# Four gather buffers instead of five, and a look-ahead of three units instead of four

## The reference

```python
x = x + _L0_conv_ref(_gn(x), ...)   # convs, scans over 1024, 256 and 64 positions, norms, gate
x = x + _L1_conv_ref(_gn(x), ...)   # 8 heads, softmax over 1024 positions
x = x + _L2_conv_ref(_gn(x), ...)   # deformable sampling, below
x = x + _L3_conv_ref(_gn(x))        # T = |u_i - u_j| * D, p <- T p twenty times, x * p
```

```python
samp = (v00 * (1 - wx) + v01 * wx) * (1 - wy) + (v10 * (1 - wx) + v11 * wx) * wy
return jnp.einsum('hwpc,hwp->hwc', samp, m)
```

## Time and profile before

| | us |
|---|---|
| median of 3 runs | 13640.77 (13637.18 to 13640.95) |
| the profiled execution | 13625.95 |
| its span, first to last instruction | 13624.3 |
| POOL busy | 9244.1 |
| DVE busy | 8980.9 |
| PE busy | 8520.4 |
| ACT busy | 4912.7 |

### The profile page before, as it was taken

The page is one execution under the profiler, slowest core; times in us unless marked ns, Lnnn a source line. Parts: engine busy times, 40 slices in busy tenths (PEclk is TensorE's granted clock), DMA queues, the critical chain, the costliest instruction groups (busy, mean ns, idle before and its releaser), DMA issues. The chain is left out here.

```text
span 13624.3 us, 109343 instructions
## 1 busy us (share of the span) xinstructions
PE 8520.4 (63%) x32752; PEld 4123.7 (30%) x32752; DVE 8980.9 (66%) x9874; ACT 4912.7 (36%) x13609; POOL 9244.1 (68%) x9221
## 2 busy tenths in 40 slices
PE   5784657456675568456675568456775558466667
PEld 3241324132332324232332324232332324222223
DVE  6755976559664886569664886569664886544443
ACT  3232643136331553146331643146331643132221
POOL 0004777777777777777777777777777777777771
PEclk7896778767887679767887679767887679787888
DMA  1002121331233112321233112421233121333221
GB/s 73 10 19 68 54 62 53 102 99 54 61 89 112 53 53 62 118 83 54 61 89 112 54 54 60 119 83 54 60 89 112 54 62 52 119 125 98 80 83 49
DMA packets 643728, 1003.96 MB, mean 74 GB/s; under 512 B 435793, under 2 KB 446033, under 8 KB 631186
## 3 DMA queue, kind: packets, MB, share of 16 engines
q0 software_dynamic: 294912, 604.57, 15.7%
q1 hardware_dynamic: 348178, 391.95, 8.4%
HBM read 814.38 MB, written 181.49 MB: 73 GB/s over the span
## 5 line engine op out<-in xcount | busy, mean ns | idle before, releaser
L133 POOL DMA_INDIRECT gat<-corner_tables,idx x9216 | 9243.7, 1003 | 4079.0 <-issue 2772.2
L151 ACT ACTIVATE gat<-gat,wts 128x32 f32<-128x32 f32 x8752 | 1919.7, 310 | 879.3 <-DMA gat<-corner_tables,idx 878.8
L166 DVE TENSOR_TENSOR gat<-gat,wts 128x1152 f32<-128x1152 f32 (+3 forms) x1024 | 1093.2, 1068 | 1634.2 <-DMA gat<-corner_tables,idx 1526.4
L804 PE MATMUL PS<-hc,ident 128*128 128x512 f32 (+2 forms) x4096 | 1922.5, 628 | 244.5 <-DVE hc L848 198.1
L172 DVE TENSOR_REDUCE dcn<-gat 128x32 f32<-128x1152 f32 x1024 | 1385.2, 1353 | 310.2 <-ACT gat L151 277.0
L871 DVE TENSOR_TENSOR_SCAN hs<-dA,PS 128x1024 f32<-128x1024 f32 x672 | 1532.5, 2280 | 45.8 <-ACT dA L821 18.1
L804 PEld LDWEIGHTS PS<-hc,ident 128*128 128x128 f32 x4096 | 983.6, 273 | 825.8 <-issue 442.4
L1159 ACT ACTIVATE E<-PS,nmax 128x1024 f32<-128x1024 f32 x512 | 570.0, 1113 | 902.3 <-DVE nmax L1216 706.0
L1080 PE MATMUL PS<-ident,E 128*128 128x128 f32 x4096 | 599.8, 294 | 395.4 <-ACT ET L1149 215.2
L848 DVE TENSOR_TENSOR hc<-hs,PS 128x1024 f32<-128x1024 f32 x672 | 802.8, 1195 | 0.8 <-PE PS L783 0.8
L1784 PE MATMUL PS<-late_M,wp 128*32 128x512 f32 x4480 | 613.5, 697 | 254.5 <-DVE wp L1825 171.3
(11 more groups left out here) (262 smaller groups left out, 11605.9 us busy)
## 6 DMA issues: line engine op xcount, KB each, us to landing
gat<-corner_tables,idx POOLq DMA_INDIRECT x9216
corner_tables<-xp SPq DMA_DIRECT2D x512, 128.0 KB, 3.0
D<-in_dist_dram SPq DMA_DIRECT2D x8, 4096.0 KB, 14.5
keep_scratch<-X SPq DMA_DIRECT2D x15, 2048.0 KB, 11.4
weighted<-M SPq DMA_DIRECT2D x56, 512.0 KB, 2.7
late_M<-weighted SPq DMA_DIRECT2D x7, 4096.0 KB
wqkv<-in_qkv_w_dram SPq DMA_DIRECT2D x8, 3072.0 KB, 11.6
X<-keep_scratch SPq DMA_DIRECT2D x12, 2048.0 KB, 16.5
```

What stands on the lines that cost most here:

```text
L133: nc.gpsimd.indirect_dma_start(bd.gat[n % self.NG][:, k * 4 * CG:(k + 1) * 4 * CG], None, bd.rows, bass.IndirectOffsetOnAxis(ap=bd.idx[:, ...
L151: ins = nc.scalar.activation(block, block, ACT.Copy, scale=weights[:, i:i + 1])
L166: nc.vector.tensor_tensor(v, v, wv, ALU.mult).then_inc(self.prod, 1)
L804: mm = nc.tensor.matmul(PS[:, p.ybank(d, h), 0:p.hl], self.ident[:], src[:, j, h * p.hl:(h + 1) * p.hl], start=(c == 0 and j == 0), stop=( ...
```

## The change

`NG` is the number of buffers `gat`, and also sets the look-ahead, `NG - 1`. It goes from 5 to 4. One buffer of 128 x 1152 fp32 values and one semaphore are left out. Every place that uses `NG` follows: the buffer of unit n is `gat[n % 4]`, the wait at tap 0 of unit n is for the reduce of unit n - 4, and a stage's part of the stream of gathers ends one unit earlier.

```diff
-    NG = 5
+    NG = 4
```

## The result

| | before | after |
|---|---|---|
| median, us | 13638.98 (13633.07 to 13640.95) | 13730.92 (13721.70 to 13739.69) |
| profiled execution | 13625.95 | 13739.69 |
| its span | 13624.3 | 13738.1 |

The ratio is 1.0071, with a 95% interval from 1.0058 to 1.0084: 92 us slower. The forecast of 13780 us had the side and the mechanism right, and was 36 to 49 us too slow.

What follows compares the result with a forecast made beforehand. POOL's chain of gathers was taken as the bound from 1150 us on. Stalls at three places summed to 139.5 us, added to 13640.8 for 13780 us; range 13745 to 13815 (chance 0.77), wider range 13725 to 13825.

Steps and rivals of the forecast that it cites:

- The bound and the rule: From 1150 us on POOL's gathers set the time; look-ahead costs nothing, but unit n really waits for unit n-4's reduce.
- rival A: Gram stage: the stall at unit 9 is absorbed in the conv stage, taking out 52 us: 13728; chance 0.08.
- place 1: Gram stage, images 1 to 7: unit 9 waits for unit 5's reduce, 4.4 to 8.6 us an image.
- Place 2: Steps into scan, images 1 to 6: unit 33 waits for unit 29's reduce, net 11.24 us; image 0, unit 19, 5.3.
- I take nothing off: Gathers stretched less after a stall: no relief in the forecast, 20 us for it in the low end.
- Rival C: Not slower: stretched gathers shrink while POOL stands still, over 112 us back; chance 0.04 same, 0.02 faster.
- Place 3: Prepare stage: unit 119 waits for unit 115's reduce, 2.3 to 2.6 us an image, none in images 0 and 7.
- The base: Median of the runs shown, 13640.8 us, 14.8 above the profiled execution, to which 139.5 us of stalls were added.
- B: Every one of 20 stalls costs a whole unit, as DVE's delay comes back to POOL: 13866; chance 0.06.
- D: Four buffers are enough, since each stall finds DVE ahead: 13641; chance 0.03.
- What would show it: Trace after: buffer waits 150 to 160 us, nearly all in 20 waits; POOL's busy time and issue within 10 us.
- The rule weighed: Skill's shared-port rule: DVE's SBUF-to-SBUF TENSOR_SCALAR holds the port GpSimd needs for descriptors; gather 2.86 us against 0.944.

Runs made afterwards that it cites:

- the second timing: The changed kernel (four buffers, look-ahead three) timed and traced again beside the five-buffer kernel before, on the same chip: 13743.8 us, ratio 1.0076.

## Why the prediction was right, and where it was off

**The bound and the rule: right.** POOL's stream sets the time from the first gather on; the experiment with 128 fewer gathers gives 0.96 us for each microsecond. The look-ahead costs nothing and the wait for the reduce is everything (1.0000 against 1.0082).

**The range: saved by a rival that did not happen.** The forecast's own range was 13745 to 13815 us, with a chance of 0.77. The measured 13730.9 lies 14 us under it, and the second timing, 13743.8, just under it. The wider range from 13725 holds both, but its lower end stood there for rival A, place 1 absorbed, which is not what happened. So the side, the mechanism and most of the size are the forecast's; that the first median fell inside the stated range is in part luck.

**Place 2: the price right, the picture incomplete.** The slip from unit 27 to 36 is 11.2 us in each of images 1 to 6, in both traces, against 11.24 forecast. Only the shape was wrong. I had found the unit that is latest against its buffer, and the late ones before it are stops as well: unit 29 first. Its buffer comes free at 6111.70 + 0.28, 5.4 us after it would have started. The four stops together are 15.02 - 4 x 0.30 = 13.8 us, less the 1.7 that the stop at unit 34 had, makes 12.1; POOL's gathers take 0.9 less in that window, and 11.2 are left. So the count of waits (50, not 20) and the size of the one at unit 33 (5.2, not the 13 that "2 to 13 us" meant for it) missed, and the sum did not.

**Place 1: the term that was mis-sized.** 52 us were forecast and 33 to 39 paid. Two things make it up. The stops at unit 9 add up to 48 us in the first trace; they are 4.4 us in images 3, 4 and 7 where 8.6, 7.9 and 8.6 were read, and larger in images 1, 5 and 6. The forecast took the reduce of unit 5 to be as late as POOL is by then. In image 3 POOL's unit 5 starts 54.7 us later than before (5820.50 against 5765.79), but DVE's reduce of it ends only 50.7 us later (5873.21 against 5822.50): the 4.0 us between them are what the stop is shorter. DVE is not in POOL's shadow here: it waits for TensorE. Here are, for image 3, 18 matmuls of L1696 in a row, DVE's wait for them, and the window of those matmuls (length, PE's busy time and count, granted clock, DMA's share and GB/s), before:

```profile
5798.55 10.68 PE L1696 MATMUL PS<-U 128*128 128x512 f32 x18
...
5808.53 1.23 DVE L1720 SCALAR_TENSOR_TENSOR fd<-PS,sqb 128x1024 f32<-128x1024 f32 x1 [9.70 <-PE PS L1696]
...
5798.55:5809.23 10.68, 10.68 (x20) 0.74 0.17 49
```

And after:

```profile
5851.95 7.99 PE L1696 MATMUL PS<-U 128*128 128x512 f32 x18
...
5859.24 1.23 DVE L1720 SCALAR_TENSOR_TENSOR fd<-PS,sqb 128x1024 f32<-128x1024 f32 x1 [7.01 <-PE PS L1696]
...
5851.95:5859.94 7.99, 7.99 (x20) 1.00 0.17 49
```

The granted clock of TensorE was 1.00 (2.4 GHz) throughout after, and at half of that (1.2 GHz) for a part of the window before. That is 2.7 of the 4.0 us, and the wait for TensorE just ahead of it (13.79 against 14.75 us) gives another 1.0. It holds for the images one by one: before, DVE's wait for L1696 is 7.01 us in images 1 and 5, the two with the smallest lateness (4.4 and 5.7 us), and 9.6 to 9.7 in the others. After, it is 7.01 in images 3, 4 and 7, where the stop is 4.4 us, 8.4 in images 2 and 5 (8.1 and 8.0) and 9.7 and 10.1 in images 1 and 6 (9.2 and 9.9). So the forecast read each stop at the clock that its image had in one execution, and the clock falls to other images in another. The rest is relief: 0.5 us in image 1 and 1.3 to 2.2 in images 2 to 7, at units 12 and 13, behind the stop.

**"I take nothing off": wrong.** I looked for relief in the unit behind the stop and found 2.2 us at most, so I left it out of the forecast and gave it 20 us in the low end. The gathers as a whole took 29.0 us less (32.1 in the second trace): about 12 us of it at the units 12 and 13, 11 us in the prepare stage, the rest spread. A stopped POOL issues later against DVE's instructions. Counting the gathers that begin while DVE multiplies by the weights (L166), there are 704 where there were 713, and they are stretched by 293.4 us in place of 307.1: 14 of the 29 us (19 of the 32 in the second trace). The rest lies beside other instructions of DVE, 6 us of it at L1712 in gram. Rival C had the mechanism, and its size was rightly held too small to turn the sign: 29 of the 112 us that it needed.

**Place 3: found, and over-priced.** Its stops are there (2.60 at unit 119, and one of 0.84 at unit 120 that was not foreseen), image 0 has one of 3.48 at unit 119 that I had not found, and the stretch costs 10 to 11 us instead of 14.8. In image 3 the stops come to 2.8 us and the gathers give 1.7 back.

**The base.** The sum of 139.5 was put on a median that lay 14.8 us above the profiled execution of before. The idle time of POOL grew by 143.9 us between the traces, 5.6 of it waits for idx. The 138 us that are left are the forecast to 2 us, which is partly luck: the stops of place 1 came to 4 us less than forecast, those of place 2 to 5 us more, and image 0 had one at unit 119 that was not in it. Less 29 of relief and plus 6 before the first gather, that is 115, and the spans of the two profiled executions are 113.8 apart. The medians are 92 and 105 apart, because the execution that was profiled before lies 13 us under its median and those after at 9 and 3 above theirs. So of the miss of 49 us against the first median, 36 against the second, about 29 is the relief, and the rest is this scatter.

**The rivals.** A (place 1 absorbed, 13728) comes closest to the first median by its number, and is not what happened. The stop is on POOL's stream and comes out as 33 to 39 us of slip, and to mend it gave 14 us where A would give nothing. B (a whole unit for each stop): no; from unit 36 to 78 of an image the slip moves by -2.3 to +4.2 us, far from a unit's 11.24. D (four are enough): no, with 172 us of waits.

**What would show it.** The buffer waits rose to 172 us, not 150 to 160. The issue time stayed within 7 us, POOL's busy time did not stay within 10. From image 2 to image 3 the start of unit 0 slips by 23.9 us more (22 forecast), but those of units 24 to 72 by 18 to 19, and of the last units by 10, so "each start by 22" missed. DVE's wait for gathers rose by 95 us, less than the sum, as foreseen.

**The rule weighed.** Rows 12 were read as a gather beside a TENSOR_SCALAR. But the gather of 2.86 us starts at 7195.23, and the TENSOR_SCALAR only at 7196.61. At the gather's start DVE was busy with an addition of two operands from SBUF (before, image 3):

```profile
7194.03 2.55 DVE L1490 TENSOR_TENSOR XN<-om,basepos 128x2304 f32<-128x2304 f32 x1
```

It ends at 7196.58, the TENSOR_SCALAR at 7197.97 and the gather at 7198.09. So the row shows both kinds of instruction together, and the agreement holds only for the end, 0.12 us after the TENSOR_SCALAR's. The last section takes up the kind with two operands, which has the larger part of the stretch.

## What to carry to other kernels

Where one engine's stream is the bound and others free its buffers, line up the start of each piece with the release of the buffer that it would need; the latest one of a run of late pieces is the price of the run, and the ones before it are part of it. A sum found in this way was above what was paid here (139.5 us against 92 to 105), though single stops came out larger than read (9.2 us for 4.4 in image 1). Look for work whose length depends on what another engine does at that moment, and expect a stop to shift it; here it gave back 29 us with four buffers and 41 with three. And where the late release hangs on TensorE, its granted clock decides how late it is, so take the spread over the images and not one image's number. The place of a buffer's release can be moved by the split of the work (43 us here with four buffers, nothing with five), but a stop removed at one place partly comes back at the next (24 us gained and 9 lost), so measure the pair on one chip before believing the cure.

## What the runs showed of the hardware

A gather on POOL takes longer if it begins while DVE multiplies two operands from SBUF. Before, image 3, gram, DVE's multiplication and the gather that begins 0.06 us after it (from the views of the two engines):

```profile
5846.84 0.95 DVE L166 TENSOR_TENSOR gat<-gat,wts 128x768 f32<-128x768 f32 x1
```

```profile
5846.90 1.71 POOL L133 DMA_INDIRECT gat<-corner_tables,idx  x1 [0.30 <-issue]
```

The multiplication ends at 5847.79, and the gather 0.82 us after that, where an undisturbed one takes 0.94 in all: it looks as if nearly all of its work waits for DVE's instruction to end. This holds all through that trace. 713 gathers begin during the multiplication L166 and take 0.43 us more on average, 307 us in all. Of them 623 begin with more than 0.16 us of it to go, and 614 of these end 0.80 to 0.84 us after its end; the other nine begin in its first 0.03 us and take the usual 0.94 or 0.95. The 1134 gathers that begin during DVE's reduce (L172, 1.35 us long, with one operand from SBUF) take 0.96 us at most. So it is not DVE's being busy that counts, but what it does, and leaving the multiplication out took 287 us off. The Trainium skill, SBUF — State Buffer, section "SBUF: two separate sides", tells of a port pair that VectorE and GpSimd share, held for a whole instruction; an instruction of VectorE with two SBUF inputs takes it only against a GpSimd operation that reads SBUF. The trace agrees if an indirect gather counts as one that reads SBUF, as it has its row numbers from `idx`; the section itself speaks of descriptor writing beside another kind of VectorE instruction.

For this kernel the detail is worth 2% of the time: DVE is busy for 66% of the span only, yet its multiplication costs 287 us of POOL's time and 308 us of the kernel's. That is more than the fifth buffer is worth (92 to 105 us).
